# Top-k search beside attention: joins of found bits with a scalar operand, and batch 0's counts in halves over two slots

## The reference, cut to what matters

```
scores = jnp.einsum('BTC,CE->BTE', x, gate_w)
probs = jax.nn.softmax(scores, axis=-1)
probs_et = jnp.transpose(probs, (0, 2, 1))
top_p, top_idx = jax.lax.top_k(probs_et, cap)        # cap = 2 * 1024 / 8 = 256
xin = jnp.take_along_axis(x[:, None, :, :], top_idx[..., None], axis=2)
```

## Time and profile before

| | us |
|---|---|
| median of 3 runs | 981.73 |
| lowest, highest | 978.76, 984.08 |
| the profiled execution, its time | 979.79 |
| its span, first to last instruction | 978.0 |
| TensorE busy | 870.7 (89%) |
| VectorE busy | 714.5 (73%) |
| ScalarE busy | 749.4 (77%) |
| GpSimd busy | 664.1 (68%) |

### The profile page before, as it was taken

The page is one execution under the profiler, slowest core; times in us unless marked ns, Lnnn a source line. Parts: engine busy times, 40 slices in busy tenths (PEclk is TensorE's granted clock), DMA queues, the critical chain, the costliest instruction groups (busy, mean ns, idle before and its releaser), DMA issues.

```text
span 978.0 us, 14970 instructions
## 1 busy us (share of the span) xinstructions
PE 870.7 (89%) x4598; PEld 734.7 (75%) x4598; DVE 714.5 (73%) x1178; ACT 749.4 (77%) x1449; POOL 664.1 (68%) x1055
## 2 busy tenths in 40 slices
PE   6899999999999999999999999999998996676550
PEld 4678888888888888888888888777787775575550
DVE  6777777777777777777777777898888865763341
ACT  4988888888888888888988788877787875533441
POOL 4676767677777677767786667666667666756862
PEclk9999999999999999999999999999999997778875
DMA  6000000000000000001020100000000022422424
GB/s 178 2 27 1 28 1 28 1 27 1 28 1 28 1 27 1 28 1 29 0 72 1 28 2 28 4 28 1 17 1 17 1 71 70 122 23 37 85 24 97
DMA packets 48766, 28.57 MB, mean 29 GB/s; under 512 B 5760, under 2 KB 46752, under 8 KB 48688
## 3 DMA queue, kind: packets, MB, share of 16 engines
q1 hardware_dynamic: 43056, 23.29, 8.3%
q0 software_dynamic: 5632, 4.33, 3.3%
HBM read 21.19 MB, written 6.42 MB: 28 GB/s over the span
## 4 chain that ended last, share of the span: by engine, by line
PE 70%; DVE 9%; issue 8%; ACT 5%; POOL 5%; DMA 2%; SPq 1%; POOLq 0%; ACTq 0%; DVEq 0%
PE t_ps L1353 10%; PE ring_b L1316 6%; PE ring_b L1318 6%; PE ring_b L1317 6%; PE ring_a L1316 5%; PE ring_a L1318 5%; PE ring_a L1317 5%; PE u_ps L1316 5%; PE u_ps L1318 5%; PE u_ps L1317 5%; PE o_ps L1316 2%; DVE negmax L916 2%; PE o_ps L1318 2%; PE o_ps L1317 2%; DVE at_lo L923 2%
## 5 line engine op out<-in xcount | busy, mean ns | idle before, releaser
L545 POOL TENSOR_TENSOR attn<-prob 128x1024 f32<-128x1024 f32 x128 | 308.1, 2407 | 192.0 <-ACT prob L688 183.3
L923 DVE TENSOR_TENSOR at_lo<-t_ps,at_hi 128x512 fp32r<-128x512 f32 x253 | 173.7, 687 | 96.5 <-ACT at_hi L671 96.5
L916 DVE TENSOR_REDUCE negmax<-ring_a 128x1 f32<-128x1024 f32 x128 | 156.5, 1222 | 57.3 <-PE ring_a L1318 55.6
L671 ACT ACTIVATE at_hi<-t_ps 128x512 fp32r<-128x512 f32 x253 | 151.4, 598 | 55.5 <-PE t_ps L1353 54.6
L1353 PE MATMUL t_ps<-ident,attn 128*128 128x128 f32 x1012 | 152.8, 273 | 16.6 <-DVE at_lo L923 16.5
L1353 PEld LDWEIGHTS t_ps<-ident,attn 128*128 128x128 f32 x1012 | 123.8, 140 | 45.8 <-DVE at_lo L923 25.8
L916 DVE TENSOR_REDUCE negmax<-ring_b 128x1 f32<-128x1024 f32 x128 | 155.9, 1218 | 1.9 <-PE ring_b L1318 0.9
L688 ACT ACTIVATE prob<-prob,coef 128x1024 f32<-128x1024 f32 x128 | 147.6, 1154 | 2.6 <-POOL coef L516 2.6
L682 ACT ACTIVATE prob<-ring_a,negmax 128x1024 f32<-128x1024 f32 x128 | 142.8, 1115 | 6.3 <-DVE negmax L916 5.8
L682 ACT ACTIVATE prob<-ring_b,negmax 128x1024 f32<-128x1024 f32 x128 | 142.3, 1111 | 1.2 <-DVE negmax L916 1.2
L1316 PE MATMUL ring_b<-xt_hi,q_hi 128*128 128x512 f32 x256 | 111.5, 436 | 2.2 <-ACT prob L682 2.2
(11 more groups left out here) (377 smaller groups left out, 1846.4 us busy)
## 6 DMA issues: line engine op xcount, KB each, us to landing
wq_s<-in_L_attn_Wq SPq DMA_DIRECT2D x16, 128.0 KB, 2.4
wk_s<-in_L_attn_Wk SPq DMA_DIRECT2D x16, 128.0 KB, 2.6
wv_s<-in_L_attn_Wv SPq DMA_DIRECT2D x16, 128.0 KB, 2.1
wvt_s<-in_L_attn_Wv_T SPq DMA_DIRECT2D x16, 128.0 KB, 2.5
wot_s<-in_L_attn_Wo_T SPq DMA_DIRECT2D x16, 128.0 KB, 2.6
raw_a<-in_L_ffn_w SPq DMA_DIRECT2D x8, 256.0 KB
attn<-in_L_ffn_w SPq DMA_DIRECT2D x8, 256.0 KB
xres<-in_L_attn_X SPq DMA_DIRECT2D x2, 512.0 KB, 8.3
```

Of the source, the lines that this page charges most:

```text
L545: pool.tensor_tensor(attn[:, t % AB, :], prob[:, t % 2, 1, :], prob[:, t % 2, 0, :], ALU.add).then_inc(attn_ready, 1)
L671: act.activation(at_hi[:, g % 2, half * GT:(half + 1) * GT, c], t_bank(t, half)[:, :].rearrange("p (k q) -> p k q", q=P), ACT.Copy).then_i ...
L916: dve.tensor_reduce(negmax[:, par, m:m + 1], ring[m][:, :], axis=AX.X, op=ALU.max, negate=True).then_inc(negmax_ready, 1)
L923: dve.tensor_tensor(at_lo[:, g % 2, k, c], t_bank(t, half)[:, :].rearrange("p (k q) -> p k q", q=P), at_hi[:, g % 2, k, c].bitcast(F32), A ...
```

## The change

The five joins (three functions) are written as `tensor_scalar`: the first operand is the tensor, the second is a per-partition scalar operand that is read from SBUF, and the operation is the same bitwise or. Both batches use them.

For batch 0, a count is cut in two instructions of 512 columns, each with an accumulator column of its own in `cnt`, now 128x2. The first is put where the whole count was, at the end of slots 100, 102, ... 114. The second is put behind `add_out` of the slot that follows, and with it `hit` (which now adds the two columns and compares in one instruction) and the joins of `level_base`. Votes and steps stay in their slots. Batch 1 keeps its count of 1024 columns.

```
-            def level_count(b, lv):
+            def level_probe(b, lv):
 
                 if lv == 0:
...
-                    probe = jtab[:, 0:1]
-                else:
-                    dve.wait_ge(cand_ready, (LEVELS - 1) * b + lv)
-                    probe = cand[:, :]
-                dve.tensor_scalar(tie[b], rows[b], probe.bitcast(F32), None, ALU.is_ge, ALU.add,
-                                  accum_out=cnt[:, :]).then_inc(cnt_ready, 1)
-                dve.wait_ge(cnt_ready, LEVELS * b + lv + 1)
-                dve.tensor_scalar(hit[:, :], cnt[:, :], CAP - 0.5, None, ALU.is_ge).then_inc(hit_ready, 1)
+                    return jtab[:, 0:1].bitcast(F32)
+                dve.wait_ge(cand_ready, (LEVELS - 1) * b + lv)
+                return cand[:, :].bitcast(F32)
+
+            def level_half(lv, h):
+
+                c = slice(h * NC, (h + 1) * NC)
+                dve.tensor_scalar(tie[0][:, c], rows[0][:, c], level_probe(0, lv), None, ALU.is_ge, ALU.add,
+                                  accum_out=cnt[:, h:h + 1]).then_inc(cnt_ready, 1)
+                if h == 1:
+                    dve.wait_ge(cnt_ready, 2 * (lv + 1))
+                    dve.tensor_scalar(hit[:, :], cnt[:, 0:1], cnt[:, 1:2], CAP - 0.5, ALU.add,
+                                      ALU.is_ge).then_inc(hit_ready, 1)
+
+            def level_count(b, lv):
+
+                dve.tensor_scalar(tie[b], rows[b], level_probe(b, lv), None, ALU.is_ge, ALU.add,
+                                  accum_out=cnt[:, 0:1]).then_inc(cnt_ready, 1)
+                dve.wait_ge(cnt_ready, 2 * LEVELS + lv + 1)
+                dve.tensor_scalar(hit[:, :], cnt[:, 0:1], CAP - 0.5, None, ALU.is_ge).then_inc(hit_ready, 1)
 
             def level_base(b, lv):
...
-                    dve.tensor_tensor(base[:, b:b + 1], base[:, b:b + 1], step[:, :],
+                    dve.tensor_scalar(base[:, b:b + 1], base[:, b:b + 1], step[:, :], None,
                                       ALU.bitwise_or).then_inc(next_ready, 1)
...
-                    dve.tensor_tensor(base_j[:, :], base[:, b:b + 1], jtab[:, lv + 1:lv + 2],
+                    dve.tensor_scalar(base_j[:, :], base[:, b:b + 1], jtab[:, lv + 1:lv + 2], None,
                                       ALU.bitwise_or).then_inc(next_ready, 1)
...
-                if G == G_COUNT:
-                    level_count(0, 0)
-                    level_base(0, 0)
-                if G in G_VOTES[:-1]:
-                    level_count(0, G_VOTES.index(G) + 1)
-                    level_base(0, G_VOTES.index(G) + 1)
+                if G in [G_COUNT, *G_VOTES[:-1]]:
+                    level_half((G - G_COUNT) // 2, 0)
+                if G - 1 in [G_COUNT, *G_VOTES[:-1]]:
+                    level_half((G - 1 - G_COUNT) // 2, 1)
+                    level_base(0, (G - 1 - G_COUNT) // 2)
```

More of the change, by code:

```diff
@@ L223, in build @@
         step = sb("step", [P, 1], I32)
-        cnt = sb("cnt", [P, 1])
+        cnt = sb("cnt", [P, 2])
         hit = sb("hit", [P, 1])
@@ L1062, in level_step @@
                     dve.wait_ge(next_ready, n + 2 * lv + 1)
-                    dve.tensor_tensor(cand[:, :], base_j[:, :], step[:, :], ALU.bitwise_or).then_inc(cand_ready, 1)
+                    dve.tensor_scalar(cand[:, :], base_j[:, :], step[:, :], None, ALU.bitwise_or).then_inc(cand_ready, 1)
                 else:
                     dve.wait_ge(next_ready, n + 2 * lv)
-                    dve.tensor_tensor(base[:, b:b + 1], base[:, b:b + 1], step[:, :],
+                    dve.tensor_scalar(base[:, b:b + 1], base[:, b:b + 1], step[:, :], None,
                                       ALU.bitwise_or).then_inc(next_ready, 1)
```

## The result

The changed kernel takes 970.9 us, the median of 4 executions (970.0 to 973.2), against 980.6 for the kernel before (978.8 to 984.1): a ratio of 0.990, with a 95% interval of 0.9875 to 0.9927. The profiled execution has a span of 968.3 us against 978.0.

A forecast was written before the change was run, and what follows sets the result against it. TensorE was taken to bound the attention loop. The span of 978.0 less 6.6 (loop waits) and 0.5 (batch 1) gives 970.9; for the median, 981.73 - 7.1 = 974.6 us, range 971.0 to 980.0.

The forecast's parts named there:

- What bounds the loop, the 8 waits and their cause: Slots 100 to 116: TensorE sets the pace; 8 waits on `at_lo`, 6.6 us, behind joins that GpSimd's addition holds.
- all 8 waits should go: -6.6 us: Ends of even slots 100 to 114: `at_lo` comes 0.7 to 1.0 us early, so TensorE's waits vanish, saving 6.6 us.
- The 17 slots should last some 101 us: Sign to look for in the profile after: attention-loop slots 100 to 116 last some 101 us.
- Joins at 0.15 us: VectorE's rewritten joins take 0.15 us, also inside GpSimd's additions; bounds 0.15 us or as before, up to 1.03.
- ScalarE's lateness: Ends of odd slots 101 to 115: VectorE's 0.95 us wait for ScalarE hides the 1.11 us of added work.
- The half counts: Batch 0's counts of 512 columns on VectorE: 0.74 us each, also inside GpSimd's additions.
- The vote: Slot after `hit`: some 0.4 us of room is left, so no cost; bound 0 to 0.2 us a slot.
- Batch 1, -0.5 us: Join of `cand` ahead of batch 1's count takes 0.67 us, 0.51 too much; the new form saves 0.5 us.
- Given back later: Rival, behind the loop: shifted tail loses 0 to 4.5 us, say 3, to clock or tie steps; 977.6 us, chance 0.14.
- The second and third rivals: Joins wait as before: 979.1 us, chance 0.08. Batch 0's half counts wait for GpSimd: 990.6 us, chance 0.04.
- the third's mechanism: On VectorE, fp32 `tensor_scalar` in SBUF can run two elements a cycle on both ports, a mode that takes the lock.

## Why the prediction was right and wrong

- **What bounds the loop, the 8 waits and their cause:** right in the main. All 8 went, and the two experiments that keep one part of the change each show waits where joins are held or the work is too long. Two of the 8 had GpSimd's subtraction behind the addition as a further cause (above), and a join was held for up to 1.29 us (`base_j` of the first level), where the prediction's bound, from one group of joins alone, was 1.03. Neither changes the sum.
- **The term "all 8 waits should go: -6.6 us" was mis-sized:** it is -8.3. I took a wait to cost the idle time that the view lists, and so put the time at which TensorE wants slot 103's `at_lo` at 631.05 - 0.61 = 630.44; by the pace without a wait it is 630.10 + 0.18 = 630.28. A wait costs its listed time and some 0.21 us, since the overlap with the work ahead is lost and the work behind passes on later. 8 x 0.21 = 1.7 us. This is the step that failed, and it alone moves the forecast to 972.9 and the range's low end to 969.3, below what was measured.
- **The rest of the miss:** the forecast lay 3.7 us above the median. 1.7 of it is this term. 1.1 is the starting value, 981.73 from three executions where four gave 980.6, which is scatter. 0.9 has no shown cause.
- **"The 17 slots should last some 101 us":** misread. The 108 us from 614 on are 16 slots and a little more. The 17 slots took 112.66 before, 106.1 less 6.6, and 104.33 was measured.
- **Joins at 0.15 us:** they aren't held, as argued, but take 0.20 to 0.22. A scalar operand from SBUF in place of a second tensor costs 0.05 us, and `hit` with two of them 0.21 instead of 0.15. The end of the odd slots took 1.28 us (634.60 to 635.88 for slot 103), not 1.11. `at_lo` came 0.24 us later behind `add_out` than before, so ScalarE's lateness didn't cover all of it; it ended at 636.56, 0.39 us ahead of the transposes at 636.95, and that room took the rest.
- **The half counts:** 0.736 us in the median, 0.74 forecast.
- **The vote:** no wait, 0.4 us of room, confirmed from the other side by the whole count in the odd slots.
- **Batch 1, -0.5 us:** not to be told from nothing. Taking the new joins out of batch 1 changed the median by +1.7 and by -0.1 us, and putting them in alone by -1.1, with an interval that reaches 0.
- **Given back later:** the tail shifts between executions, and its clock with it. From the start of slot 127 to the end of the span the three traces of the changed kernel have 188.6, 193.6 and 188.3 us. The two with the old loop (before, and before with new joins in batch 1) have 191.8 and 191.7, and whether that one differs between executions of the kernel before was not seen. This rival had a chance of 0.14 and a price of +3. No loss shows in the medians.
- **The second and third rivals** don't hold here, but the third's mechanism is real for a form of instruction that the change doesn't have.

The medians moved by 9.7, 12.6 and 9.0 us in three comparisons, and the loop accounts for 8.3. The mean of the 16 executions of the changed kernel is 970.7, 9 to 10 us below the means of the kernel before beside them. Some 1 to 2 us stay without a shown cause; no effect of batch 1's joins of that size shows, and they are within the scatter of the tail. That starting the tail 8 us earlier gains something there was not tested.

## What to carry to other kernels

Look in VectorE's timeline for small instructions with long durations beside a GpSimd instruction on two tiles in SBUF. Here those with two tensors in SBUF (a 128x1 join: 0.16 us alone, up to 1.6), and `tensor_scalar` of one tensor of 256 columns without an accumulator (0.35 us alone, 1.52), stood until GpSimd had ended. A scalar operand in place of the second tensor of one column, an accumulator output of `tensor_scalar`, and a place in the slot where GpSimd's addition doesn't run each took the wait away. And count a short wait of TensorE in a loop like this one as its listed idle time and some 0.2 us more; a delay too short to be listed cost up to 0.35 us.

## What the runs showed of the hardware that was not expected

- `tensor_scalar` over 256 columns of fp32 in SBUF took 0.35 to 0.43 us alone and 1.5 to 2.5 beside GpSimd's addition; with an accumulator output it took 0.48 beside it.
- Not every GpSimd instruction holds a join of two tensors: in the trace before, one of 0.16 us started at 630.23 and ran inside GpSimd's 128x1 power (`rs`, L508, 630.14 to 630.69).
- The hold works the other way too. In the changed kernel's trace an addition that starts 0.09 us behind a VectorE instruction with two tensors takes 2.85 us instead of 2.40 (in the version with the tie steps moved, where that instruction stands elsewhere, it doesn't):

```profile
753.88 0.68 DVE L1128 TENSOR_TENSOR xg<-cumg,grp 128x512 bf16<-128x512 bf16 x1
```

```profile
753.97 2.85 POOL L545 TENSOR_TENSOR attn<-prob 128x1024 f32<-128x1024 f32 x1 [2.93 <-ACT prob L688]
```

- A wait of TensorE ahead of the transposes costs 0.20 to 0.24 us beyond its listed idle time.
- Slots repeat to 0.02 us between executions, while a stretch of 72 slots with a granted clock of 1.00 throughout took between 430.4 and 432.2 us in different executions of all kernels.
